# Max pass of an exact-softmax attention in head pairs on two row halves of TensorE, with one job per step and one job bank

## What is computed

```python
xn = layer_norm(x, norm_w, norm_b)
q = (xn @ q_w + q_b).reshape(Bx, Tx, H, -1)
k = (xn @ k_w + k_b).reshape(Bx, Tx, H, -1)
att = jnp.einsum('bnhl,bmhl->bnmh', q, k)
att = jax.nn.softmax(att + (1.0 - mask) * -1000000.0, axis=2)
v = ((xn @ v_w + v_b) * src_mask[:, :, None]).reshape(Bx, Tx, H, -1)
y = jnp.einsum('bnmh,bmhl->bnhl', att, v).reshape(Bx, Tx, Dx)
e = jax.nn.silu(emb) @ emb_w + emb_b
scale, shift = jnp.split(e[:, None, :], 2, axis=2)
h = layer_norm(y, sb_norm_w, sb_norm_b) * (1.0 + scale) + shift
return x + jax.nn.silu(h) @ out_w + out_b
```

## Time and profile before

| | before |
|---|---|
| median of 3 runs | 563.6 us (562.95 to 565.53) |
| profiled execution, its own time | 566.29 us |
| its span, first to last instruction | 564.2 us |
| granted TensorE clock, mean | 0.991 of 2.4 GHz |
| PE busy | 542.6 us (96%) |
| DVE busy | 435.3 us (77%) |
| ACT busy | 370.8 us (66%) |
| POOL busy | 192.9 us (34%) |
| max reductions on DVE | 512, 328.9 us |
| exps on ACT | 512, 278.5 us |
| DMA | 53.74 MB, mean 95 GB/s |

### The profile page before, as it was taken

How to read it: one execution, slowest core, us unless ns; L and a number is a source line. 1 busy time by engine, 2 the same in 40 slices (tenths; PEclk the granted TensorE clock), 3 DMA queues, 4 the chain that set the end, 5 groups by cost and what they waited for, 6 DMA issues and landing times.

```text
span 564.2 us, 10272 instructions
## 1 busy us (share of the span) xinstructions
PE 542.6 (96%) x2831; PEld 226.1 (40%) x2834; DVE 435.3 (77%) x914; ACT 370.8 (66%) x674; POOL 192.9 (34%) x238
## 2 busy tenths in 40 slices
PE   6899999999999999999999999999999999998986
PEld 3452334334443344434443344434443344422333
DVE  7299777987869868897869878797869878787525
ACT  2305866777757786687756886677756786675851
POOL 6432302346205522336205422336114432314003
PEclk9989999999999999999999999999999999998999
DMA  5650242332225343242235243242334232241021
GB/s 137 191 164 17 82 123 86 102 107 85 70 85 143 87 112 105 74 139 84 73 94 138 81 119 104 60 137 80 84 102 130 85 85 85 66 142 41 1 76 37
DMA packets 43433, 53.74 MB, mean 95 GB/s; under 512 B 11000, under 2 KB 36728, under 8 KB 43408
## 3 DMA queue, kind: packets, MB, share of 16 engines
q1 hardware_dynamic: 41360, 53.17, 33.1%
q10 hardware_dynamic: 2048, 0.27, 0.3%
HBM read 36.35 MB, written 16.80 MB: 94 GB/s over the span
## 4 chain that ended last, share of the span: by engine, by line
PE 73%; issue 7%; DVE 6%; DMA 5%; SPq 3%; POOL 3%; ACT 2%; POOLq 0%; ACTq 0%; DVEq 0%
PE pv_ps L428 18%; PE mx_ps L395 17%; PE st_ps L412 16%; PE job_ps L470 7%; PE job_ps L504 4%; PE job_ps L477 4%; DMA q_rows<-qk_dram 4%; DVE negmax L711 3%; PE job_ps L492 2%; SPq L1088 2%; POOL qk_parts L964 1%; ACT probs L550 1%; SPq L1091 1%; PE job_ps L487 1%; PE pv_ps L352 1%
## 5 line engine op out<-in xcount | busy, mean ns | idle before, releaser
L711 DVE TENSOR_REDUCE negmax<-mx_ps 128x1 f32<-128x512 f32 x512 | 328.9, 680 | 76.2 <-PE mx_ps L395 72.6
L550 ACT ACTIVATE probs<-st_ps 128x512 f32<-128x512 f32 x512 | 278.5, 598 | 99.2 <-PE st_ps L412 98.5
L395 PE MATMUL mx_ps<-k_rows,q_rows 99*128 99x512 bf16 x512 | 197.0, 385 | 7.1 <-DMA q_rows<-qk_dram 6.3
L412 PE MATMUL st_ps<-q_rows,k_rows 101*128 101x512 bf16 x512 | 194.2, 382 | 2.8 <-ACT probs L550 1.2
L428 PE MATMUL pv_ps<-probs,v_rows 128*32 128x512 f32 x1024 | 137.0, 607 | 0.5 <-ACT probs L550 0.5
L395 PEld LDWEIGHTS mx_ps<-k_rows,q_rows 99*128 99x128 bf16 x512 | 50.6, 99 | 126.6 <-DVE negmax L711 82.6
L955 POOL TENSOR_TENSOR qk_rest<-qk_full,qk_parts 128x512 f32<-128x512 f32 x32 | 37.1, 1159 | 163.4 <-ACT qk_parts L560 163.4
L412 PEld LDWEIGHTS st_ps<-q_rows,k_rows 101*128 101x128 bf16 x512 | 49.9, 98 | 62.6 <-ACT probs L550 23.4
L964 POOL TENSOR_TENSOR qk_parts<-qk_rest,qk_parts 128x512 bf16<-128x512 f32 x32 | 37.1, 1160 | 69.6 <-DVE qk_parts L788 68.6
L470 PE MATMUL job_ps<-x_norm_t,w_qk 128*128 128x512 f32 x128 | 60.7, 596 | 0.0
L571 ACT ACTIVATE qk_full<-job_ps,qkb_col 128x512 f32<-128x512 f32 x32 | 22.0, 687 | 37.9 <-PE job_ps L470 37.9
(11 more groups left out here) (94 smaller groups left out, 392.5 us busy)
## 6 DMA issues: line engine op xcount, KB each, us to landing
qk_dram<-qk_parts SPq DMA_DIRECT2D x96, 128.0 KB
k_rows<-qk_dram SPq DMA_DIRECT2D x32, 192.0 KB
q_rows<-qk_dram SPq DMA_DIRECT2D x32, 192.0 KB
x_in<-in_x SPq DMA_DIRECT2D x16, 256.0 KB, 3.5
k_rows<-qk_dram SPq DMA_DIRECT2D x32, 128.0 KB
q_rows<-qk_dram SPq DMA_DIRECT2D x32, 128.0 KB
x_res<-in_x SPq DMA_DIRECT2D x8, 512.0 KB, 4.5
out<-out_sb SPq DMA_DIRECT2D x16, 256.0 KB, 2.2
```

The costliest lines, as they stand in the source:

```text
L395: pe.matmul(mx_ps[bank_of(u, MX_BANKS)][:, :], q_rows[0:ROWS_MASK, g, h, c * P:(c + 1) * P], k_rows[0:ROWS_MASK, g, h, :], start=True, sto ...
L412: pe.matmul(st_ps[bank_of(u, ST_BANKS)][:, :], k_rows[0:ROWS_ALL, g, h, c * P:(c + 1) * P], q_rows[0:ROWS_ALL, g, h, :], start=True, stop= ...
L550: act.activation(probs[:, t % P_SLOTS, h, :], st_ps[bank_of(u, ST_BANKS)][:, :], ACT.Exp).then_inc(exp_done, 1)
L711: dve.tensor_reduce(negmax[:, g % 2, h * CH + c:h * CH + c + 1], mx_ps[bank_of(GH * step + h, MX_BANKS)][:, :], AXIS_X, ALU.max, negate=Tr ...
```

## The change

- **Max pass.** It uses three of the six products (the two largest parts) and the three mask rows: 51 partitions. The product rows are laid out anew: partitions 0 to 50 hold mask and three products for heads 0 and 1, partitions 64 to 114 those for heads 2 and 3; the other three products of a head stand in the other half, and the two rows of the maximum lie at partitions 51 and 52. A max matmul runs on one half of the rows (`tile_position=(64 * half, 0)`), so heads j and j + 2 form a pair on both halves. `st` reads 115 partitions.
- **Banks.** Four max banks as two pairs (was three single), one job bank (was two). DVE reduces a pair with one instruction of 128x1024.
- **Order of a step on PE:** two `st`, the turn of the maxima if there is one, pv, all four max matmuls, two `st`, one job. The maxima are taken seven steps ahead. The turn goes to a max bank, at steps 1, 5, 9 and 13, and the second pair of that step waits for DVE's split.
- **Jobs.** One a step, in a table by step; a job waits for the reader of the job before it. In the body ahead of batch 0 they use several banks, and projection 3 of batch 0 is done there.
- **Spreading.** SP saves four copies (part 0 twice), waits for all, and issues eight fills of 48 partitions and two heads each. Two mask DMAs instead of one. SP also places the maxima (was ACT).
- **POOL and DVE.** x's norm for batch b + 2 is at the end of the body (was b + 1 at its start); statistics and late reads of jobs are at other steps, by tables. Half of `q_rows` and `k_rows` presets are larger memsets.

The core of the diff:

```diff
-MAX_LEAD = 6
+MAX_LEAD = 7
+PAIRS = GH // 2
...
-MX_BANKS = 3
-JOB_BANKS = 2
...
-ROWS_PROD = 6 * HD
-ROWS_MASK = ROWS_PROD + PARTS
-ROWS_ALL = ROWS_MASK + 2
+COPIES = PARTS + 1
+HALF = P // 2
+ROWS_PROD = 3 * HD
+ROWS_MX = PARTS + ROWS_PROD
+ROW_MAX = ROWS_MX
+ROWS_ALL = HALF + ROWS_MX
...
 JOBS = [
-    (0, END, "yturn", 3, -1), (1, END, "proj", 3, 0), (2, MID, "cturn", 1, 0), (3, END, "xturn", 0, 1),
...
+    ("yturn", 3, -1), ("xturn", 0, 1), ("xturn", 1, 1), ("proj", 0, 1),
+    ("hturn", 0, -1), ("vproj", 0, 1), ("yturn", 0, 0), ("proj", 1, 1),
+    ("hturn", 1, -1), ("vproj", 1, 1), ("yturn", 1, 0), ("proj", 2, 1),
+    ("yturn", 2, 0), ("outp", 0, -1), ("outp", 1, -1), ("proj", 3, 1),
 ]
+TURNS = {1: 1, 5: 2, 9: 3, 13: 4}
+LATE = {(2, 0): (15, -1), (5, 0): (3, 0), (7, 2): (4, 0), (9, 0): (7, 0), (10, 2): (8, 0), (13, 0): (11, 0)}
...
-        mx_ps = [psum(f"mx_ps{i}", [P, T]) for i in range(MX_BANKS)]
+        mx_ps = [psum(f"mx_ps{i}", [P, 2, T]) for i in range(PAIRS)]
         pv_ps = psum("pv_ps", [P, T])
-        job_ps = [psum(f"job_ps{i}", [P, T]) for i in range(JOB_BANKS)]
+        job_ps = psum("job_ps", [P, T])
...
-                u = GH * step + h
-                wait(pe, max_done, UNITS * mb + bank_before(u, MX_BANKS) + 1)
-                pe.matmul(mx_ps[bank_of(u, MX_BANKS)][:, :], q_rows[0:ROWS_MASK, g, h, c * P:(c + 1) * P],
-                          k_rows[0:ROWS_MASK, g, h, :], start=True, stop=True).then_inc(max_ready, 1)
+                for j in range(PAIRS):
+
+                    wait(pe, max_done, PAIRS * (STEPS * mb + step - 1) + j + 1)
+                    if j == 1 and turn_at(b, t):
+
+                        turn, turn_b = turn_at(b, t)
+                        pe.wait_ge(max_split, NG * turn_b + turn + 1)
+                    for half in range(2):
+                        base, h = HALF * half, PAIRS * half + j
+                        pe.matmul(mx_ps[j][:, half, :], q_rows[base:base + ROWS_MX, g, h, c * P:(c + 1) * P],
+                                  k_rows[base:base + ROWS_MX, g, h, :], start=True, stop=True,
+                                  tile_position=(base, 0)).then_inc(max_ready, 1)
+
+            def max_turn(b, t):
+
+                if not turn_at(b, t):
+                    return
+                i, d = turn_at(b, t)
+                pe.wait_ge(max_done, PAIRS * CH * (NG * d + i + 1))
+                pe.transpose(mx_ps[1][0:GH * CH, 0, 0:P], negmax[:, i % 2, :], ident[:, :]).then_inc(turned["cturn"], 1)
...
             def body(b):
                 for t in range(STEPS):
...
+                    st_unit(b, t, 0)
+                    st_unit(b, t, 1)
+                    max_turn(b, t)
+                    pv_step(b, t)
+                    max_quad(b, t)
...
+                    st_unit(b, t, 2)
+                    st_unit(b, t, 3)
+                    job(t, b)
...
+                dve.tensor_reduce(by_pair[:, :, j, c], mx_ps[j][:, :, :], AXIS_X, ALU.max, negate=True).then_inc(max_done, 1)
...
+                    read_job(b, t - 1)
+                    late_job(b, t, 0)
+                    stats_at(b, t, 0)
+                    split_max(b, t)
+                    max_pair(b, t, 0)
+                    stats_at(b, t, 1)
+                    max_pair(b, t, 1)
+                    late_job(b, t, 2)
+                    stats_at(b, t, 2)
...
+                if exists(d):
+                    sp.wait_ge(copies_saved, 16 * COPIES * (n + 1))
+                    for half in range(2):
+                        at = HALF * half + PARTS
+                        for own in range(2):
+                            heads = slice(PAIRS * own, PAIRS * (own + 1))
+                            for side, rows in enumerate((q_rows, k_rows)):
+                                sp.dma_start(rows[at:at + ROWS_PROD, i, heads, :].rearrange("p h t -> p (h t)"),
+                                             copies(i, side, own, half != own)).then_inc(rows_filled[i], 16)
```

More of the change, by code:

```diff
@@ L335, in run @@
                 body(b)
-        last_ps = [[mx_ps[0], mx_ps[1]], [mx_ps[2], st_ps[1]]]
+        last_ps = [[mx_ps[i][:, k, :] for k in range(KD)] for i in range(2)]
+        last_out = [job_ps, st_ps[1]]
         def last_body(b):
@@ L897, in body @@
                     last_rows()
-            def nth_stats(b, which):
-                if not isinstance(b, int):
-                    return 2 * b + which
-                return sum(exists(i + 1) + exists(i - 1) for i in range(-1, b)) + (which if exists(b + 1) else 0)
-            run(dve, body)
+            run(dve, body, B - 2)
         @block.gpsimd
@@ new lines, in copies, with place_max @@
+            def copies(i, side, own, rest):
+                heads = slice(side * GH + PAIRS * own, side * GH + PAIRS * (own + 1))
+                of = qk_dram[i, rest:rest + PARTS, :, heads, :].rearrange("s l h t -> l s (h t)")
+                return of if side == 0 else of[:, ::-1]
+            def place_max(b, i):
+                if not turn_at(b, TURN_OF[i]):
+                    return
+                g, d = turn_at(b, TURN_OF[i])
+                sp.wait_ge(max_split, NG * d + g + 1)
+                for part in range(2):
+                    sp.dma_start(q_rows[ROW_MAX + part:ROW_MAX + part + 1, g, :, :].rearrange("p h (c t) -> p (h c) t", t=P),
+                                 max_parts[:, g % 2, part:part + 1, :]).then_inc(max_filled[g], 16)
```

415 lines of the change are left out of this document (201 added, 214 removed).

## The result

| | before | after |
|---|---|---|
| median | 563.6 us (562.95 to 565.53) | 575.7 us (574.75 to 576.93) |
| profiled execution, its own time | 566.29 us | 575.16 us |
| its span | 564.2 us | 573.4 us |
| first pv | 47.49 | 56.54 |
| first pv to last pv | 499.4 | 499.6 |

The ratio is 1.021 (95% interval 1.0177 to 1.0243): the change makes the kernel slower.

What follows compares the result with a forecast made beforehand. PE's work was taken to bound the kernel (63.87 of 64 us). First to last pv +8.6 and the start +7 made +15.6: 581.9 for the profiled execution, which stood 2.7 above the median, so 579 (562 to 596).

Steps and rivals of the forecast that it cites:

- the start: Time up to the first pv: claimed to come at about 54.5 against 47.49, +7 us (bounds +4 to +9).
- The cost of a quad: PE time of a step's four max matmuls as two pairs: 0.60 us against 0.88 before, case range 0.5 to 0.75.
- Short: Step without a long job: the 2.88 chain of st and exps plus the 0.60 quad, 3.48 us from pv to pv.
- Long: Step with a projection, value or output projection: 3.70 plus the 0.60 quad, 4.30 us from pv to pv.
- Turn: Steps 0, 4, 8 and 12, ending in the turn of the maxima: wait for both DVE reductions, 4.2 us, 3.4 before.
- A batch: Four turn, four short and eight long steps: 65.1 us against 63.9, 65.4 with the stall for rows.
- the wait for rows: Stall in each batch for group 3's rows, landing at 21.2 but wanted at 20.7: 0.3 us taken, 0 to 1 possible.
- the tightest group: Group 3, projected at step 15, its rows wanted by step 5's quad at 20.7 and landing at 21.2.
- Two more quads at 2.3: Start term: two more quads at 2.3 us, with warm matmuls and projection 3 (1.72), put the first score at 50.7.
- PE's work decides: Rival: exps and reductions overlap, PE's work sets the batch at 59.0 us, the whole at 533; chance 0.11.
- the switch costs nothing: Rival: the quad on PE costs 0.44 us, the whole 565, no change that can be told; chance 0.12.
- pairs run one after another: Rival: the pairs on PE do not run together, the quad costs 1.04 us, the whole 619; chance 0.06.

Runs made afterwards that it cites:

- half reductions: The changed kernel with DVE reducing only the first 256 of 512 keys of each max bank; 563.4 us, 0.9997 of before.
- late quad of the short steps: Kernel with one pair ahead of pv in steps 0, 4, 8, 12, plus the quad behind the two st in steps 1, 2, 6, 10; 573.1 us.
- six-ahead kernel: The changed kernel with maxima taken six steps ahead, not seven, and turned at steps 2, 6, 10 and 14; 569.5 us, 1.0109 of before.
- full rows: The changed kernel with max matmuls reading all 115 rows one after another, exps taken of zero times the score; 609.2 us.

## Why the prediction was right

It said 579 (562 to 596), slower with a chance of 0.76; the time is 575.7. The waits that it named are there and take back PE's gain. That they take back more, so that a batch gets longer by 1.5 us, did not come true: its own sign of being right, a batch of 65 to 66, failed with 64.3. The slowdown is nearly all the start.

**What of the number is luck.** Between the profiled executions it forecast +15.6 (581.9) and +8.9 came (575.2): the start was 2.0 too cheap, and from first to last pv it was 8.4 too dear. As a median it then took off the 2.7 by which before's profiled execution stood above its median; that of the change stands 0.6 below. This step was wrong by 3.3 the other way and brought 579 to within 3.3 of the time.

**The cost of a quad.** Predicted 0.60, measured 0.53, between the full overlap (0.44) and my value. By the span that the Trainium skill gives, page TensorE: Matmul & The Clock Gate, part on packing small matmuls (one matmul and some 4 ns for each further tile), it would have been 0.44; the trace has 0.09 more, once a quad. The run with the quad between st and the job shows where it comes from: there a change from one layout of tiles to another costs 0.10 on either side of the quad (0.54 for 0.44, 1.83 for 1.73). So next to pv, which hands over in 1.00 to either layout, one such change is added, and elsewhere two. My 0.09 to 0.14 for it was right; the rest that I added on top was not there.

**The steps.** Short: predicted 3.48, measured 3.42. Long: 4.30 and 4.23. Turn: 4.2 and 4.08. The reductions were priced well, 1.21 for a single one and 1.14 in a row against a mean of 1.22 and 2.36 for two. That DVE is what ends the turn step, with ACT's chain and the turn 0.2 ahead of it, is shown by the half reductions: 4.08 falls to 3.86, no further. The name of what ends it next is read from that trace (ACT without a gap behind the projection, the second st waiting for its exp); no run shortened ACT's chain.

**A batch.** 65.4 predicted, 64.3 measured. Per batch: quad 0.07 too dear in twelve steps (-0.8), turn steps (-0.5), the wait for rows, 0.3, that did not come (-0.3), and one wait that I had put under pv's cover and that lay outside it, the second pair of the output step for the split (+0.46). In six batches that is 6.8, and 1.6 in batch 0, so of the +8.6 from first to last pv only +0.2 are there.

**The fills.** A save's landing was taken as 3.73. In the batches' chain it is 2.0, as the row below shows, and 2.88 at the start. With 1.7 less the tightest group's rows land ahead of the quad that wants them, which fits that no wait for them is seen in most batches.

```profile
293.76 2.02 DMA qk_dram<-qk_parts
```

The late quad of the short steps showed how little was left: 0.5 us of lateness on DVE gave a wait of 0.54 for exactly that group.

**The start.** Predicted +7 (4 to 9), measured +9.05. First max matmul 31.3 predicted, 31.81 found. Here too errors met: 27.77 - 1.0 + 4.2 is 31.0 and not 31.3; SP issued the last fill at 29.10, not at 27.8, its first save being 1.3 later than before where I had the projection 1.0 earlier; and that fill landed in 2.67, not in 3.5. First score 50.7 predicted and 52.64 found, first pv 54.5 and 56.54. The term that was mis-sized is "Two more quads at 2.3", with what stands ahead of it. The starts of the quads are 31.81, 35.02, 37.34, 40.41, 43.50, 46.64 and 49.16. The fifth comes 1.0 later than the 42.5 at which I had its rows, and then follow 3.14 and 2.52. The first gap, 3.21, is at the lower clock level. The third and fourth gap, 3.07 and 3.09, have waits for DVE's reductions in them (0.38, 0.29), and the fifth, 3.14, the turn and the wait for the split (second pair at 44.34, 0.45 of it idle). So neither DVE nor PE's row of 2.5 sets the pace alone: the second pair waits for DVE, and warming matmuls and embedding stand behind it. The six-ahead kernel gives the price of one quad (2.4 to 2.6).

**The rivals.** That PE's work decides (533) fell: short steps wait for exps 0.5 each, and stayed at 3.42 in every kernel in which the quad lies between pv and st (3.75 on full rows, where the quad is 0.34 longer). That the switch costs nothing (565) and that pairs run one after another (619) fell by the quad's 0.53, against 0.87 on full rows.

**Where the expected gain went.** Without waits a step would be pv 1.00, quad 0.53, four st 0.96 and the job, and a batch 16 x 2.49 + 17.9 for the jobs with the turns at 0.11 + 0.4 for the rest of the turns, 0.20 each = 58.1. The 6.2 us up to 64.3 are three waits. The steps ahead of a turn have 4.08 for 3.13 of work, so 3.8 in four; the half reductions took 0.22 from each, which is DVE's part, and the other 0.73 is, as read from the trace, ACT's chain of two reads, y_t and four exps behind a projection. The short steps have 3.42 for 2.93, so 2.0, because two score banks and bursts of two st leave the exps uncovered (a quad behind the two st brought such a step down to 3.09, where nothing else was late). The second pair's wait for the split is 0.46, some 0.3 of it idle time in the row shown. Before, waits were 0.7 a batch. That a part of the ACT chain ends those steps next was in the prediction; how much of the 2.0 a third score bank would return stays open, since all eight banks are in use.

## What to carry to other kernels

When the engine that bounds a kernel gets less work, write down for each kind of step what will end it next and sum the steps, not the work: here 5.6 us less work a batch gave 0.3 us more time. Tiles of different layout should stand side by side, and a producer whose reader is long (a pair ahead of pv) is worth moving even at the price of one more change of layout. A pipeline that is a step deeper pays for it at the start: here 2.4 us for one quad with its warming matmuls and embedding. And where the profiled execution stands off its median, ask which of the two the forecast starts from, and whether what sets them apart will be there after the change.
